# A decoder layer on one core: linear attention's steps in another order, output weights centred on GpSimd, the first middle norm computed in pairs 0 and 4 of the last batch

## The chip, the cores and the metric

The kernel runs as one launch on 1 core of one Trainium2 chip. The metric is the device time of that core in microseconds (us), the median of three runs. Engines are named as in the profile: PE is TensorE's matmul side and PEld its weight load, DVE is VectorE, ACT is ScalarE, POOL is GpSimd, SP is SyncE, which here issues most DMAs (its DMA queue stands as SPq in the rows).

## The reference, cut to what matters

One decoder layer with three blocks, each followed by a layer norm without gain or bias; x is 8 batches of 512 tokens with 256 features, float32.

```python
def linear_attention(x):                 # chunks of C = 32 tokens
    Q, K, V = x @ W_q.T, x @ W_k.T, x @ W_v.T
    S = einsum('bncd,bnkd->bnck', Qc, Kc) * mask      # decay ** (i - j) for i >= j
    O = einsum('bnck,bnkd->bncd', S, Vc).reshape(B, T, D)
    return sigmoid(x @ W_g.T) * O @ W_o.T + x

def cross_attention(x, ctx):             # 16 heads of 64
    qw, kw, vw = x @ Wq + bq, ctx @ Wk + bk, ctx @ Wv + bv
    a = softmax(where(key_mask, qw @ kw.T / sqrt(64), -inf))
    return (a @ vw) @ Wo + bo

def bitlinear(x, w):                     # ternary weights
    scale = clip(mean(abs(w), axis=1, keepdims=True), 1e-05)
    return x @ (clip(round(w / scale), -1, 1) * scale).T

def ffn(x):                              # hidden 1024, low rank 16
    h = bitlinear(x, w_fc) + gate * (x @ v.T @ fast_b.T @ u.T)
    return bitlinear(relu(h) ** 2, w_proj)

x = layernorm(x + linear_attention(x))
x = layernorm(x + cross_attention(x, ctx))
x = layernorm(x + ffn(x))
```

## The kernel before

Features stand on the 128 partitions (two tiles of 128, `DK` = 2) and the 512 tokens of a batch on the free axis, so most tiles are 128x512 or 128x1024. Products of float32 quality are made of three products of rounded parts (`_hi`, `_lo`: a CAST gives the high part, a subtraction the low one). PSUM is used as eight banks of 128x512, `ps[:, 0]` to `ps[:, 7]`. Every engine runs its own hand-written program, in the order in which its calls stand in the code; semaphores with counts are the only link between them. Nothing is scheduled by a planner.

The program has three stages.

**Linear attention**, to about 170 us. Query and key weights are folded into one matrix M, so that scores are x M x. PE runs `step(b)` once a batch: gates of b (`gates`), query side (`queries`), output projection of b - 1 (`outputs`), `scores`, `values`, the mean of b - 1 (`mean`: a product with a matrix of 1/256), `attend` (chunk products into the banks QO), and the variance of b - 1 (`variance`). In `step` of DVE stand: `finish_y` (y = 2x + attention, two operations by feature tile, and their sum `tile_sum`), `mask_scores`, `subtract_mean`, `sum_squares`, `split_x` (x of b + 1 into x_hi, x_lo), `gated` (gate times attention, then split), `root` and `scale_x1` (the norm of b - 1). ACT has `front(b)` (sigmoid of the gates, then the copies `qm` of the query side), `square`, `values` (the copies `v_tok` out of PSUM, in two halves) and `deviation` (logarithm, exponential, square: the estimate of the root). The sigmoid stands in another table of ACT than those three, so each step has two table loads. SP loads x of batch b once y of b - 2 has freed its buffer, and stores x1 of earlier batches. POOL splits the weights of the next stage and makes the effective feed-forward weight in two halves (L399 to L403).

Into these steps the weights of the feed-forward are mixed: `scales` needs the sums of absolute weights (`psc`, `scale`) and the products of `scale_means` (L748 to L758 on PE), `low_rank`, `compare_in` and `compare_out` follow in single steps. `psc` is the reduction of the output weight, 128x256<-128x2048 (its row names the shared buffer `wfc`). PE waits for a small copy of DVE for `low_rank` (`f_mid`) ahead of step 1.

**Cross attention**, about 170 to 1125 us: 8 batches of 8 pairs of heads (`PAIRS` = 8, `HALF` = 4), some 12 us a pair. In pair g PE makes `key_scores` of g in four tiles of 128 keys, the maxima's scores of g + 1 (`max_scores`), `weighted_values`, `sums` of g - 1, and keys and queries two pairs ahead. ACT makes the exponentials, the copies `pvc` and the high parts, DVE the maxima (`nmx`), reciprocals and low parts, POOL the sums over the key tiles (`acc`, `acc_hi`, `acc_lo`). `project` multiplies four pairs with the output weight; it stands in pair 4 for pairs 0 to 3 and in pair 0 of the next batch for pairs 4 to 7, and DVE's `projected_out` adds the residual. The output weight `wo` is centred once, at the start of the stage: a reduction to `wo_sum` and one subtraction, both on DVE (L1242 to L1245), and split by POOL in pairs 1 and 4 of the first batch (`split_output_weight`). `first_maxima` are the maxima of the very first pair.

**Feed-forward**, about 1125 to 1316 us. `class` members with a 2 in the name make the middle norm: `norm2_square`, `sum_squares2`, `var2_first` (the variance product of batch 0, in bank 2), `norm2_root`, `root2`, `scale2`, `split2_hi` and `split2_lo` (its output cx_hi, cx_lo). For batch 0 these stand in the last batch of cross attention: square and sum in pair 2, the rest in pair 6. `weights_hi` and `weights_lo` split the feed-forward weight, `ternary` (POOL, L184) casts the ternary output weight. `rs` at L225 is the first operation of `root2`, and PE waits for it ahead of `key_scores(g, p, 1)` of the last pair, since it frees bank 2. The rest of cross attention (`last_sums`, `last_reciprocal`, `last_attended_hi`, `last_attended_lo`, `last_project`, `last_projected`) stands between the hidden tiles of feed-forward batch 0. Each batch has eight hidden tiles on four banks (`hidden`), and then `project` over them.

The only thing that sets this order is the code of the steps. `attend` waits for both value copies (`v_out`), which ACT makes behind `square(b - 1)`; the sigmoid of b waits for `gate_used`, which DVE's gate product (L576) signals.

## Time and profile before

| | |
|---|---|
| median of 3 runs | 1316.46 us (1314.57 to 1319.1) |
| the profiled execution | 1318.03 us, its span 1315.9 us, mean granted clock 0.986 |
| PE busy | 1272.9 us, 6836 instructions |
| DVE busy | 923.5 us |
| ACT busy | 794.7 us |
| POOL busy | 775.7 us |
| HBM | 32 GB/s over the span |

The span is what the profiler sees from the first to the last instruction; the execution's own time is 2.1 us longer.  [...]

### The profile page before, as it was taken

Reading aid. Unit: us, or ns where it says so; the run is one execution under the profiler, and the core shown is the slowest. Engines: PE = TensorE matmul, PEld = TensorE weight load, DVE = VectorE, ACT = ScalarE, POOL = GpSimd, SP = SyncE. Lnnn points to the kernel's source line nnn. Section 1 sums busy time; section 2 is a strip of 40 time slices with the busy share of each in tenths; the row PEclk is TensorE's granted clock in tenths of the full one; section 3 lists DMA queues with packets and bytes.
Section 4 is the critical chain, followed back from the end, with each engine's and each line's share of the span. In section 5 each row is a group of like instructions: output and inputs, shape, how many; then the busy total and the mean of one; then the engine's idle time right before and its main releaser. Section 6 shows DMA issues by size and latency. Waiting matters only on the chain.

```text
span 1315.9 us, 21104 instructions
## 1 busy us (share of the span) xinstructions
PE 1272.9 (97%) x6836; PEld 850.6 (65%) x6836; DVE 923.5 (70%) x1809; ACT 794.7 (60%) x1063; POOL 775.7 (59%) x449
## 2 busy tenths in 40 slices
PE   6999999999999999999999999999999998899997
PEld 5767765657566656665666666657566655577775
DVE  6678876684766677576757656684775677678887
ACT  2354445574656566565657565575666666679885
POOL 3504218995877687677958767794876787300000
PEclk9999998999999999999999999999999999899998
DMA  6311211100100110011011001100200110010101
GB/s 214 113 35 62 82 47 20 19 2 17 42 11 1 32 34 0 16 32 18 0 28 37 2 0 48 18 0 16 48 2 0 33 33 2 20 61 33 64 17 48
DMA packets 99392, 43.08 MB, mean 33 GB/s; under 512 B 77169, under 2 KB 82049, under 8 KB 99345
## 3 DMA queue, kind: packets, MB, share of 16 engines
q1 hardware_dynamic: 98528, 39.33, 12.1%
q0 software_dynamic: 816, 3.15, 0.7%
q8 instruction: 27, 0.44, 0.1%
q14 instruction: 21, 0.16, 0.0%
HBM read 29.59 MB, written 12.58 MB: 32 GB/s over the span
## 4 chain that ended last, share of the span: by engine, by line
PE 89%; POOL 3%; DVE 3%; ACT 2%; issue 1%; SPq 1%; DMA 1%; POOLq 0%; ACTq 0%; DVEq 0%
PE ps L1310 16%; PE ps L1285 14%; PE ps L48 11%; PE ps L50 10%; PE ps L49 10%; PE ps L1301 4%; PE ps L1289 4%; PE ps L1343 2%; PE ps L1344 2%; PE ps L1342 2%; PE ps L1319 2%; PE ps L1732 2%; PE ps L1733 2%; POOL acc L931 2%; PE ps L716 1%
## 5 line engine op out<-in xcount | busy, mean ns | idle before, releaser
L1139 DVE CUSTOM_DVE_ANT_0 junk<-ps,mask 128x512 bf16<-128x512 f32 x504 | 314.9, 686 | 89.3 <-PE ps L1301 88.0
L1005 ACT ACTIVATE prob<-ps,mcol 128x1024 f32<-128x1024 f32 x256 | 282.0, 1116 | 140.1 <-PE ps L1289 135.2
L931 POOL TENSOR_TENSOR acc<-acc,prob 128x1024 f32<-128x1024 f32 x128 | 307.0, 2399 | 11.6 <-ACT prob L1005 0.3
L928 POOL TENSOR_TENSOR acc<-prob 128x1024 f32<-128x1024 f32 x64 | 155.3, 2426 | 220.8 <-ACT prob L1005 219.5
L1310 PE MATMUL ps<-prob,v_b 128*64 128x512 f32 x1024 | 246.2, 602 | 0.0
L945 POOL TENSOR_TENSOR acc_lo<-acc,acc_hi 128x1024 f16<-128x1024 f32 x64 | 138.7, 2168 | 5.1
L1310 PEld LDWEIGHTS ps<-prob,v_b 128*64 128x64 f32 x1024 | 68.1, 137 | 108.8 <-issue 75.9
L1285 PE MATMUL ps<-q_hi,k_hi 64*128 64x512 f32 x512 | 115.1, 445 | 4.2 <-DVE rs L225 4.0
L1301 PE MATMUL ps<-k_hi,q_hi 64*128 64x512 f32 x504 | 101.0, 396 | 3.8 <-DVE nmx L1139 3.8
L1285 PE MATMUL ps<-q_hi,k_lo 64*128 64x512 f32 x512 | 102.3, 395 | 0.0
L1285 PE MATMUL ps<-q_lo,k_hi 64*128 64x512 f32 x512 | 102.1, 394 | 0.0
L1289 PE MATMUL ps<-shift,ones_r 64*128 64x512 f32 x512 | 102.0, 394 | 0.1
L1150 DVE TENSOR_TENSOR ps<-ps,recip 128x512 f32<-128x512 f32 x64 | 44.6, 697 | 67.6 <-ACT recip L1020 67.6
L1012 ACT ACTIVATE pvc<-ps 128x512 f32<-128x512 f32 x64 | 38.3, 599 | 81.2 <-PE ps L1310 81.1
L1285 PEld LDWEIGHTS ps<-q_hi,k_hi 64*128 64x128 f32 x512 | 48.4, 185 | 55.4 <-issue 27.0
L1163 DVE SCALAR_TENSOR_TENSOR att_lo<-ps,bv,att_hi 128x512 fp32r<-128x512 f32 x64 | 48.0, 751 | 48.7 <-ACT att_hi L1028 48.7
L1173 DVE SCALAR_TENSOR_TENSOR q_lo<-ps,bq,q_hi 128x512 fp32r<-128x512 f32 x64 | 48.0, 751 | 30.3 <-ACT q_hi L1036 29.6
L1042 ACT ACTIVATE v_b<-ps 128x512 f32<-128x512 f32 x64 | 38.3, 598 | 50.0 <-PE ps L50 50.0
L1036 ACT ACTIVATE q_hi<-ps,bq 128x512 fp32r<-128x512 f32 x64 | 44.1, 688 | 37.5 <-PE ps L50 37.4
L941 POOL CAST acc_hi<-acc 128x1008 f16<-128x1008 f32 x64 | 65.4, 1022 | 0.0
L1028 ACT ACTIVATE att_hi<-ps,bv 128x512 fp32r<-128x512 f32 x64 | 44.1, 689 | 33.3 <-DVE ps L1158 33.3
L1301 PEld LDWEIGHTS ps<-k_hi,q_hi 64*128 64x128 f32 x504 | 47.8, 185 | 19.0 <-DVE nmx L1139 4.9
(230 smaller groups left out, 2881.9 us busy)
## 6 DMA issues: line engine op xcount, KB each, us to landing
shift<-nmx SPq DMA_DIRECT2D x512, 0.5 KB, 2.0
x_in<-in_xT SPq DMA_DIRECT2D x8, 512.0 KB, 3.7
x_scratch<-x_a SPq DMA_DIRECT2D x8, 512.0 KB, 2.8
raw<-in_cT SPq DMA_DIRECT2D x8, 512.0 KB, 3.7
raw<-x_scratch SPq DMA_DIRECT2D x8, 512.0 KB, 3.9
y<-x_scratch SPq DMA_DIRECT2D x8, 512.0 KB, 3.7
y_scratch<-y SPq DMA_DIRECT2D x8, 512.0 KB, 2.8
y_c<-y_scratch SPq DMA_DIRECT2D x8, 512.0 KB, 3.8
```

What stands on the lines that cost most here:

```text
L48: pe.matmul(out, lh, rh, start=(i == 0), stop=False)
L49: pe.matmul(out, lh, rl, start=False, stop=False)
L50: mm = pe.matmul(out, ll, rh, start=False, stop=(i == n - 1))
L928: pool.tensor_tensor(total, prob[:, 0], prob[:, 1], ALU.add).then_inc(acc_out, 1)
L931: pool.tensor_tensor(total, total, prob[:, kt], ALU.add).then_inc(acc_out, 1)
L945: pool.tensor_tensor(acc_lo[:], acc[:], acc_hi[:], ALU.subtract).then_inc(sum_lo_out, 1)
L1005: act.activation(prob[:, i].rearrange("p h t -> p (h t)"), SCORE[i % 2].rearrange("p h t -> p (h t)"), ACT.Exp, scale=SCALE, bias=mcol[:, ...
L1139: dve.tensor_tensor_reduce(junk[:, t % 2, h], SMAX[t % 2][:, h], mask[:], -1.0, -LOWEST, ALU.add, ALU.min, nmx[:, p % 2, t, h:h + 1]).then ...
L1285: pe.matmul(banks[:, h], l[OWN[h], par, cols], r[OWN[h], par], start=(n == 0), stop=False)
L1289: mm = pe.matmul(banks[:, h], ones_r[OWN[h], :], shift[OWN[h], par], start=False, stop=True)
L1301: mm = pe.matmul(SMAX[t % 2][:, h], q_hi[OWN[h], par, toks], k_hi[OWN[h], par], start=True, stop=True)
L1310: mm = pe.matmul(PV[OWN[h], :], v[:, kt, cols], prob[:, kt, h, :], start=(kt == 0), stop=(kt == NT - 1))
```

## The change

No product is added or removed. What moves:

- **Linear attention, PE.** The first gates are made in three parts as x_hi, then x_lo are there (`first_gates`). `variance(b - 2)` stands behind the gates of step b; `scale_means` goes from behind step 1 into step 2, between gates and queries. Values come in two halves, (0, 1) and (2, 3), and `attend` takes the first half of its tiles when the first half of the value copies is there. The wait for `f_mid` goes from ahead of step 1 to ahead of its `mean`.
- **Linear attention, ACT.** `front` keeps the sigmoid alone, followed at once by the load of the other table; then `deviation(b - 2)`, the query copies, the values, and last the square.
- **Linear attention, DVE.** `root(b - 2)` opens the step, `scale_x1(b - 2)` and `split_x(b + 1)` come behind `mask_scores`, ahead of `subtract_mean`. The reduction `psc` (`sum_out_weights`) goes from ahead of step 1 into step 1, behind `gated(1)`. Stores of x1 come one batch later.
- **First pair.** The reduction `wo_sum` and the new `wo_mean` go between the second and the third `first_maxima`; the subtraction is made by POOL in two halves (`centre_output_weight`), and the first half of the weight is split ahead of batch 0.
- **Last batch.** `weights_hi`, `weights_lo`, `norm2_square` and `sum_squares2` of feed-forward batch 0 go to pair 0, `var2_first`, `norm2_root`, `root2`, `scale2` and `split2_hi` to pair 4, `split2_lo` to the last pair. The variance uses bank 3; its buffers are separate tiles (`first_sq`, `first_sum`, `first_rs`), and PE waits for `rs2_out` in pair 5. `ternary` goes from pair 6 to the last pair.
- **Feed-forward batch 0.** `last_sums` stands behind hidden tile 4, `last_project` behind the first four tiles of the first projection; `last_project` uses banks 3 and 6.

```diff
-        self.STAT2_FIRST, self.STAT2, self.STAT3 = ps[:, 2, :], ps[:, 0, :], ps[:, 5, :]
+        self.STAT2_FIRST, self.STAT2, self.STAT3 = ps[:, 3, :], ps[:, 0, :], ps[:, 5, :]
...
                 act.wait_ge(gate_used, b)
             act.activation(gate[:], G, ACT.Sigmoid).then_inc(g_out, 1)
+            if not (isinstance(b, int) and b < 2):
+                act.preload_act_table_set("natural_log_exp_and_others")
...
-            if not (isinstance(b, int) and b == 0):
-                act.preload_act_table_set("natural_log_exp_and_others")
...
-        values(0)
+        front(1)
+        query_copies(1)
         act.wait_ge(f_sum, 1)
         act.activation(wabs[:].rearrange("p k (j n) -> p (k j) n", n=D), wpr[:], ACT.Abs).then_inc(f_abs, 1)
-        front(1)
+        values(1)
         square(0)
-        values(1)
-        deviation(0)
         with act.Fori(2, B - 1, 2) as i:
...
                 front(b)
+                deviation(b - 2)
+                query_copies(b)
+                values(b)
                 square(b - 1)
-                values(b)
-                deviation(b - 1)
...
+        la.deviation_late = lambda: deviation(B - 2)
...
         def step(b, par, last):
+            if b > 1:
+                root(b - 2)
             finish_y(b - 1, 1 - par)
             mask_scores(b)
+            if b > 1:
+                scale_x1(b - 2)
+            if not last:
+                split_x(b + 1, 1 - par)
             subtract_mean(b - 1)
             sum_squares(b - 1)
-            if not last:
-                split_x(b + 1, 1 - par)
             gated(b)
             if b == 1:
+                sum_out_weights()
                 scales()
             if b in (2, 3):
                 low_rank(b - 2)
-            if not last:
-                root(b - 1)
-                scale_x1(b - 1)
             if b in (3, 4):
                 compare_in(b - 3)
             if b in (5, 6):
...
+        split_x(1, 1)
         mask_scores(0)
-        split_x(1, 1)
-
+        gated(0)
         dve.wait_ge(f_abs, 1)
         dve.tensor_tensor(scale[:], wabs[:, 0], wabs[:, 1], ALU.add).then_inc(f_sum, 1)
-        gated(0)
         dve.wait_ge(f_mid_ps, 1)
         dve.tensor_copy(mid[:], ST[0:RANK, 0:D]).then_inc(f_mid, 1)
-        dve.wait_ge(f_abs, 2)
-        dve.tensor_reduce(psc[:], wabs[:].rearrange("p k (j n) -> p n (k j)", n=D), AX.X, ALU.add).then_inc(f_sum, 1)
...
-                for t in range(NT):
-                    mm = pe.matmul(QO[:, m, t * P:(t + 1) * P], v[:, t, m * P:(m + 1) * P], s[:, t],
-                                   start=True, stop=True)
+            for n in range(2):
+                pe.wait_ge(v_out, 2 * b + n + 1)
+                for m in range(DK):
+                    for t in (2 * n, 2 * n + 1):
+                        mm = pe.matmul(QO[:, m, t * P:(t + 1) * P], v[:, t, m * P:(m + 1) * P], s[:, t],
+                                       start=True, stop=True)
                 mm.then_inc(o_ps, 1)
...
+        def first_gates():
+            for l, r, ready in ((w_hi, x_hi, 1), (w_lo, x_hi, 1), (w_hi, x_lo, 2)):
+                pe.wait_ge(x_split, ready)
+                for m in range(DK):
+                    for k in range(DK):
+                        mm = pe.matmul(G[:, m], l["WgT"][:, k, m * P:(m + 1) * P], r[:, 0, k],
+                                       start=(l is w_hi and r is x_hi and k == 0), stop=(r is x_lo and k == DK - 1))
+            mm.then_inc(g_ps, 1)
...
+        first_gates()
...
+        pe.wait_ge(w_in, 32)
+        values(0, 0, (0, 1))
         scores(0, 0)
-        pe.wait_ge(w_in, 32)
-        values(0, 0, range(NT))
+        values(0, 0, (2, 3))
...
+            if b > 1:
+                variance(b - 2)
+            if b == 2:
+                scale_means()
             queries(b, par)
             if b == 2:
...
@@ -735,11 +770,15 @@
                 pe.wait_ge(f_low, b - 2)
             outputs(b - 1)
             scores(b, par)
-            values(b, par, (0,))
+            values(b, par, (0, 1))
+            if b == B - 1:
+                values(b, par, (2, 3))
+            if b == 1:
+                pe.wait_ge(f_mid, 1)
             mean(b - 1)
...
-            variance(b - 1)
 
...
-        pe.wait_ge(f_mid, 1)
         for b in range(1, B):
             step(b, b % 2)
-            if b == 1:
-                scale_means()
...
+        def centre_output_weight(half):
+            rows = slice(half * HALF, half * HALF + HALF)
+            means = wo_mean[:, rows].rearrange("p (k o) -> p k o", o=1).to_broadcast([P, HALF, D])
+            pool.wait_ge(wo_summed, 2)
+            pool.tensor_tensor(wo[:, rows], wo[:, rows], means, ALU.subtract).then_inc(wo_centred, 1)
+
...
-                if first and p in (1, HALF):
-                    split_output_weight(p // HALF)
+                if first and p == HALF:
+                    split_output_weight(1)
...
-                if last and p == PAIRS - 2:
+                if last and p == PAIRS - 1:
...
+        centre_output_weight(0)
+        pool.wait_ge(la.y_out, 2 * B)
+        split_output_weight(0)
+        centre_output_weight(1)
...
-                    f.norm2_square(act, 0, 0)
-                if last and p == PAIRS - 2:
-                    f.weights_hi(act)
...
-                if last and p == PAIRS - 2:
-                    f.norm2_root(act, 0, True)
...
+                if last and p == 0:
+                    f.weights_hi(act)
+                    f.norm2_square(act, 0, 0)
+                if last and p == HALF:
+                    f.norm2_root(act, 0, True)
...
+        la.deviation_late()
...
-                    f.weights_lo(dve, 0)
+                if last and p == PAIRS - 1:
+                    f.split2_lo(dve, 0, 0)
...
+                if last and p == 0:
+                    f.weights_lo(dve, 0)
+                    f.weights_lo(dve, 1)
+                    f.sum_squares2(dve, 0, True)
                 if p == 0 and not first:
...
+                    projected_out(b - 1, 1)
+                if last and p == HALF:
+                    f.root2(dve, 0)
+                    projected_out(b, 0, (0,))
+                    f.scale2(dve, 0, 0)
+                    projected_out(b, 0, (1,))
+                    f.split2_hi(dve, 0, 0)
+                elif p == HALF:
...
+        first_maxima(1)
+        dve.tensor_reduce(wo_sum[:], wo[:], AX.X, ALU.add).then_inc(wo_summed, 1)
+        dve.wait_ge(wo_summed, 1)
+        dve.tensor_scalar(wo_mean[:], wo_sum[:], 1.0 / D, None, ALU.mult).then_inc(wo_summed, 1)
+        first_maxima(2)
+        first_maxima(3)
         la.root(B - 1)
         la.scale_x1(B - 1)
-        dve.tensor_reduce(wo_sum[:], wo[:], AX.X, ALU.add).then_inc(wo_centred, 1)
-        dve.wait_ge(wo_centred, 1)
-        dve.scalar_tensor_tensor(out=wo[:], in0=wo_sum[:].rearrange("p (k o) -> p k o", o=1).to_broadcast([P, PAIRS, D]),
-                                 scalar=-1.0 / D, in1=wo[:], op0=ALU.mult, op1=ALU.add).then_inc(wo_centred, 1)
...
-                if last and p == PAIRS - 1:
+                if last and p == HALF + 1:
                     pe.wait_ge(f.rs2_out, 1)
...
-                if last and p == PAIRS - 2:
-                    f.var2_first(pe)
...
+                if last and p == HALF:
+                    f.var2_first(pe)
...
+            for i in (2, 3, 4):
+                hidden(b, i, first)
+            if first:
+                ca.last_reciprocal_estimate()
+            hidden(b, 5, first)
             if first:
                 ca.last_attended_hi()
-            for i in (3, 4, 5):
...
-            if first:
-                ca.last_reciprocal()
...
             hidden_lo(b, 2)
-            if first:
-                ca.last_attended_lo()
...
+            if first:
+                ca.last_reciprocal()
             hidden_lo(b, 5)
             if first:
-                ca.last_projected()
+                ca.last_attended_lo()
...
+                if first:
+                    ca.last_projected(0)
                 f.scale2(dve, b + 1, 1 - par)
             hidden_lo(b, 6)
+            if first:
+                ca.last_projected(1)
...
-            if first:
-                ca.last_sums()
-            for i in (1, 2, 3):
+            for i in (0, 1, 2, 3):
...
             if first:
+                ca.last_sums()
...
-            if first:
-                ca.last_project()
...
             if first:
-                pe.wait_ge(ca.o_out, 2 * DK * B)
...
+                for m in range(DK):
+                    project(b, m, range(0, 4))
+                pe.wait_ge(f.relu_out, 6)
+                ca.last_project()
+                for m in range(DK):
+                    project(b, m, range(4, 6))
...
+            if first:
+                pe.wait_ge(ca.o_out, 2 * DK * B)
```

Three places, by the order of the instructions on an engine. First DVE, one step of linear attention (b = 3): `x_hi`, `x_lo` are the split of x, `dev_a` the mean subtraction, `tile_sum_a<-sq_a` the sum of squares, `sq_a<-ps,gate` the gate product, `rs_a` the root. Before:

```order
L523 SCALAR_TENSOR_TENSOR y_a<-x_in,ps 128x512 x2
L528 TENSOR_TENSOR tile_sum_a<-y_a 128x512
L547 TENSOR_TENSOR s_masked<-ps,dmask 128x512
L541 TENSOR_TENSOR dev_a<-y_a,ps 128x1024
L533 TENSOR_TENSOR tile_sum_a<-sq_a 128x512
L481 CAST x_hi<-x_in 128x1024
L483 TENSOR_TENSOR x_lo<-x_in,x_hi 128x1024
L576 TENSOR_TENSOR sq_a<-ps,gate 128x1024
L578 CAST og_hi<-sq_a 128x1024
L580 TENSOR_TENSOR og_lo<-sq_a,og_hi 128x1024
```

With the change, from the root of the batch before the last:

```order
L571 SCALAR_TENSOR_TENSOR rs_a<-ps,eps,inv_a 128x512
L574 SCALAR_TENSOR_TENSOR rs_a<-rs_a,est_a 128x512
L539 SCALAR_TENSOR_TENSOR y_a<-x_in,ps 128x512 x2
L544 TENSOR_TENSOR tile_sum_a<-y_a 128x512
L563 TENSOR_TENSOR s_masked<-ps,dmask 128x512
L581 SCALAR_TENSOR_TENSOR x_a<-dev_a,rs_a 128x1024
L497 CAST x_hi<-x_in 128x1024
L499 TENSOR_TENSOR x_lo<-x_in,x_hi 128x1024
L557 TENSOR_TENSOR dev_a<-y_a,ps 128x1024
L549 TENSOR_TENSOR tile_sum_a<-sq_a 128x512
L592 TENSOR_TENSOR sq_a<-ps,gate 128x1024
L594 CAST og_hi<-sq_a 128x1024
```

The split of x stands ahead of the mean subtraction instead of behind the sum of squares, and the root ahead of y instead of behind the gate product.

Second POOL, at the start of cross attention; `bx` is the split input, `acc` the sum over key tiles of the first pair. Before:

```order
L985 CAST bx_hi<-raw 128x1024
L949 TENSOR_TENSOR bx_lo<-raw,bx_hi 128x1024
L988 MEMSET shift 128x1024
L928 TENSOR_TENSOR acc<-prob 128x1024
L931 TENSOR_TENSOR acc<-acc,prob 128x1024 x2
```

With the change:

```order
L1031 CAST bx_hi<-raw 128x1024
L989 TENSOR_TENSOR bx_lo<-raw,bx_hi 128x1024
L1034 MEMSET shift 128x1024
L999 TENSOR_TENSOR wo<-wo,wo_mean 128x1024
L1004 CAST wo_hi<-wo 128x1024
L1006 TENSOR_TENSOR wo_lo<-wo,wo_hi 128x1024
L999 TENSOR_TENSOR wo<-wo,wo_mean 128x1024
L968 TENSOR_TENSOR acc<-prob 128x1024
```

Four operations on the output weight stand ahead of the first sum.

Third DVE in the last batch of cross attention: `x`, `x_even` is the output of the middle norm, `cx_hi`, `cx_lo` its split. Before, from the low weights in pair 6 on, into its norm:

```order
L1150 TENSOR_TENSOR ps<-ps,recip 128x512
L1152 SCALAR_TENSOR_TENSOR ps<-ps,recip 128x512
L1158 SCALAR_TENSOR_TENSOR ps<-pvc,ps 128x512
L1163 SCALAR_TENSOR_TENSOR att_lo<-ps,bv,att_hi 128x512
L180 TENSOR_TENSOR wfc_lo<-wfc,wfc_hi 128x1024
L225 SCALAR_TENSOR_TENSOR rs<-ps,eps,inv 128x512
L228 SCALAR_TENSOR_TENSOR rs<-rs,est 128x512
L238 SCALAR_TENSOR_TENSOR x<-y_c,rs 128x1024
L245 CAST cx_hi<-x 128x1024
L249 TENSOR_TENSOR cx_lo<-x,cx_hi 128x1024
```

With the change, in pair 4:

```order
L1218 SCALAR_TENSOR_TENSOR k_lo<-ps,bk,k_hi 128x512
L1223 SCALAR_TENSOR_TENSOR q_lo<-ps,bq,q_hi 128x512
L240 SCALAR_TENSOR_TENSOR first_rs<-ps,eps,first_sq 128x512
L243 SCALAR_TENSOR_TENSOR first_rs<-first_rs,first_sq 128x512
L1234 SCALAR_TENSOR_TENSOR y<-ps,bo_centred,y 128x512
L253 SCALAR_TENSOR_TENSOR x_even<-y_even,first_rs 128x1024
L1234 SCALAR_TENSOR_TENSOR y<-ps,bo_centred,y 128x512
L260 CAST cx_hi_even<-x_even 128x1024
```

The norm lies between the two additions of the projection's result; nothing of it but the last subtraction (`split2_lo`) is left for the last pair.

## Rows read from the trace of the kernel before

**Rows 1.** Page, part 1: busy us, share of the span, instructions.

```profile
PE 1272.9 (97%) x6836; PEld 850.6 (65%) x6836; DVE 923.5 (70%) x1809; ACT 794.7 (60%) x1063; POOL 775.7 (59%) x449
```

**Rows 2.** Waits of PE, whole span: waiting, awaited: total us, times, longest.

```profile
PE ps L716 <- ACT v_tok L437: 7.1, 8, 1.0
...
PE ps L1285 <- DVE rs L225: 4.0, 1, 4.0
PE ps L1301 <- DVE nmx L1139: 3.8, 2, 2.9
PE ps L48 <- issue: 3.5, 1, 3.5
...
PE ps L1319 <- DVE att_lo L1163: 1.9, 1, 1.9
PE ps L1319 <- POOL acc_lo L945: 1.7, 1, 1.7
...
PE ps L48 <- DVE cx_lo L249: 1.4, 1, 1.4
```

**Rows 3.** Windows after waits: length, busy of PE, PEld, DVE, ACT, POOL, PEclk, DMA.

```profile
198.00:206.00 8.00, 7.07 (x24) 3.07 (x26) 4.63 (x16) 1.11 (x1) 7.50 (x5) 0.57 0.13 10
1115.00:1121.00 6.00, 5.90 (x28) 4.36 (x30) 5.93 (x3) 3.02 (x4) 6.00 (x3) 0.59 0.01 3
1131.00:1138.00 7.00, 6.59 (x18) 4.94 (x19) 3.78 (x6) 4.77 (x8) 0.35 (x1) 0.57 0.00 0
```

**Rows 4.** Timeline, start of linear attention: start us, duration us, instruction.

```profile
30.22 3.83 DVE L640 TENSOR_REDUCE psc<-wfc 128x256 f32<-128x2048 f32 x1
...
50.15 1.88 PE L753 MATMUL ps<-scale,mean_w 128*128 128x512 f32 x4
```

**Rows 5.** Timeline of SP: issues of x for batches 3, 6 and 7.

```profile
62.00 0.39 SPq L360 DMA_DIRECT2D x_in<-in_xT  x1
...
121.78 0.38 SPq L360 DMA_DIRECT2D x_in<-in_xT  x1
...
139.85 0.38 SPq L360 DMA_DIRECT2D x_in<-in_xT  x1
```

**Rows 6.** Tile x_in, all its loads.

```profile
DMA to landing us min/median/max: 3.3/3.7/8.3
```

**Rows 7.** Timeline of DVE, inside one step of linear attention.

```profile
128.09 0.68 DVE L481 CAST x_hi<-x_in 128x1024 fp32r<-128x1024 f32 x1
128.81 1.23 DVE L483 TENSOR_TENSOR x_lo<-x_in,x_hi 128x1024 fp32r<-128x1024 f32 x1
129.95 1.22 DVE L576 TENSOR_TENSOR sq_a<-ps,gate 128x1024 f32<-128x1024 f32 x1
...
133.85 0.69 DVE L558 SCALAR_TENSOR_TENSOR rs_a<-rs_a,est_a 128x512 f32<-128x512 f32 x1
```

**Rows 8.** Timeline of ACT, the same step.

```profile
125.69 1.06 ACT L432 ACTIVATE sq_a<-dev_a 128x1024 f32<-128x1024 f32 x1 [6.88 <-DVE dev_a L541]
...
131.51 0.63 ACT L448 ACTIVATE est_a<-inv_a 128x512 f32<-128x512 f32 x1
...
132.82 1.28 ACT L421 ACT_TABLE_LOAD   x1
```

**Rows 9.** Timeline near 102 us: DVE beside POOL's weight step.

```profile
102.20 2.35 POOL L401 TENSOR_TENSOR wfc_raw<-wfc_raw,scale 128x1024 f32<-128x1024 f32 x1
102.26 2.83 DVE L528 TENSOR_TENSOR tile_sum_a<-y_a 128x512 f32<-128x512 f32 x1
```

**Rows 10.** Timeline of DVE, the first pair's maxima and the reduction.

```profile
187.15 0.69 DVE L1145 CUSTOM_DVE_ANT_0 junk<-ps,mask 128x512 bf16<-128x512 f32 x1 [2.54 <-PE ps L1295]
...
193.05 2.28 DVE L1242 TENSOR_REDUCE wo_sum<-wo 128x8 f32<-128x2048 f32 x1
```

**Rows 11.** Timeline, last batch: ACT in pair 0, POOL in pair 6.

```profile
1035.01 4.68 ACT L1005 ACTIVATE prob<-ps,mcol 128x1024 f32<-128x1024 f32 x4 [5.88 <-PE ps L1289]
...
1116.13 2.35 POOL L184 CAST tern_r<-tern 128x2048 fp32r<-128x2048 bf16 x1
```

171 lines of the change are left out of this document (87 added, 84 removed).

## The prediction

> **What bounds the kernel now.** I read the page first: TensorE (PE) is busy for 97% of the span [rows 1], so only its idle time and its slow time can be won. Second, the waits of PE [rows 2]: 7.1 us in eight waits of 0.9 us for the value copies of linear attention, 3.5 us once at the start ("issue": PE stood at the semaphore f_mid), 2.9 of the 3.8 us for `nmx` at the first pair, 0.9 of them in pair 3 of the last batch, 4.0 us for `rs` in the last pair, and 1.4, 1.9 and 1.7 us at the start of the feed-forward stage. Between the first pair and the last batch PE never waits, and that code is unchanged. [...] Busy time times (1 - clock) is what each costs: 7.07 x 0.43 = 3.0 us after the first-pair wait, 5.90 x 0.41 = 2.4 after the wait for `rs`, 6.59 x 0.43 = 2.8 after the feed-forward waits. Waits of 0.9 us leave the clock alone.
>
> The change has three parts that can be summed apart.
>
> **Linear attention, start.** The first gates begin on x_hi alone, copies come before the weight means, and PE no longer stands at f_mid: by the measured durations PE gets to its second attend some 7 us sooner. But the reduction of the output weights moves from before step 1 to behind `gated(1)`, and `scale_means` needs it. It takes 3.83 us [rows 4]. It now starts after y of batch 0 (by the same durations at about 33 us), the load of x for batch 2 (3.8 us with its issue, [rows 5, 6], more if it shares the DMA engines with the 1 MB weight load that GpSimd starts at that time), its split (2.0), mean subtraction, square and sum (3.1), `gated` (3.3): about 46 us, and ends at about 50. Before, `scale_means` began at 50.15 [rows 4]. So PE arrives early and waits some 6 us there, then runs slowly for a while (2 us, like those of [rows 3]). What it has then already done (2.75 us of gates) pays for that: outputs(1) ends some 0.5 us sooner than before. I take -0.5, range -2.5 to +1.
>
> **Linear attention, the loop.** The 0.9 us wait goes: values are copied before the square, and attend takes them in halves. PE alone would then need 18.07 - 0.9 = 17.2 us a step, 18.07 being the distance of two x loads [rows 5]. But the new order closes a ring through four engines, which I sum from y(b-1) to y(b). The x load, 3.8 us from its release to its landing ([rows 6] has 3.7 over all loads, from the issue); split of x, now ahead of the mean subtraction, 0.68 + 1.23; subtraction 1.22 like the op of its size; square 1.06 on ScalarE; sum 0.69; gate product 1.22 [rows 7, 8]: with hand-overs 10.0 us. The sigmoid table load carries the wait for `gate_used` in the new order as in the old, and stood clear of it before. Now it comes right at it: table 1.28, sigmoid 1.05 like the square of its size, the second table 1.28, then deviation(b-1), three functions of 0.63 [rows 8], 5.6 us. Then root's two and the two y operations, 0.69 each, 2.8 us [rows 7]. The ring is 18.4 us, longer than PE's 17.2, and longer than the 18.07 of before. PE's wait moves from attend to scores (query copies stand behind the deviation).
> Two rounds hold a low-rank product on PE (1.8 us, like the mean products of [rows 4]). The first is PE's: 19.0. In the next three GpSimd's weight steps get into the ring. [rows 9] shows the price: a 0.69 us sum lasted 2.83 us, until GpSimd's 2.35 us operation beside it had ended. Two-input SBUF operations of the ring (root's second, tile_sum, scale_x1) now meet such operations, 1.3 to 1.6 us a round: 19.7, 20.0, 20.0. The last is 18.5. The same four rounds took 139.85 - 62.00 = 77.9 us before [rows 5]; now 78.7; with the fifth +1.3 us. In the last step there is no x load and the ring is open: its value-copy wait of 0.9 us goes [rows 2], and GpSimd's splits of the next stage's inputs, which held its gate split, are over sooner, worth 0.9 more (half of one hold as in [rows 9]): -1.8. Linear attention together: -0.5 + 1.3 - 1.8 = **-1.0**, range -9 (ring never binds: five rounds at PE's pace) to +4 (twice the holds).
>
> **First pair.** Reduction (2.28 us) and means go into VectorE's idle 2.54 us before the third maximum [rows 10], and the 2.3 us subtraction to GpSimd. The maxima are due 4.6 us earlier, which would remove 2.9 us of wait and the 3.0 us of clock. But GpSimd now runs about 8 us of subtraction and splitting just while VectorE does root's second operation and scale_x1. By [rows 9] each can be held for one GpSimd operation: up to 3 us, so the maxima start 1.1 instead of 4.6 us earlier and 1.9 us of wait stay. [...] I take the middle of 0 and 1.9: 1.0 us of wait and half of the clock loss. **-5.9 + 2.5 = -3.4**, range -5.9 to -1.
>
> **Last batch and feed-forward.** Weights, square and sum go to pair 0. There ScalarE is idle for 5.88 us while PE projects [rows 11]; they need 3.1. VectorE gets 3.2 us more before the y additions; the first ends about when PE asks for its bank: 0 to 0.3 us. In pair 4 the variance product costs PE 0.9 us (half of the two-product row in [rows 4]), the same that it saves in pair 6; root and scale hide behind the 24 products of the projection. Gone: 0.9 + 4.0 + 1.4 + 1.9 + 1.7 = 9.9 us of waits, 5.2 us of clock. What is late next: with no product ahead of it the last pair waits 0.8 us for the `pvc` copy, and its second score tile 0.8 us for att_lo of the pair before, both formerly hidden; exponentials pace the short pair (0.5). GpSimd ends its sums about 6.6 us after PE has begun the hidden tiles; the ternary copy, 2.35 us [rows 11], comes right behind. VectorE's hidden_lo and sum_squares2 have only SBUF inputs and alternate with them, so PE stands at var2(1): 0.5 us if nothing is held, 3.1 if twice. I take 2.4. The last projection then starts with its inputs ready, and batch 1 follows without a wait. **-15.1 + 4.5 = -10.6**, range -13.5 to -6.5 (the clock falls once more).
>
> **Sum.** -1.0 - 3.4 - 10.6 = -15.0. The profiled execution took 1318.03 us (span 1315.9), 1.6 above the median; it would be 1303.0, and against the median 1316.46 - 15.0 = **1301.4 us**.
>
> **Rivals.**
> (A) The ring doesn't bind, because loads land in 3.3 us and sigmoid's table is loaded while waiting: linear attention gives -8 instead of -1: 1294. For it: 18.4 against 17.2 is only 1.2 us, half of it hand-overs. Against: each piece is a measured row.
> (B) Holds and clock cost more: a fresh slow stretch in the last pair or at var2 (2.4 to 2.8 us), the first pair keeps its wait, linear attention loses 3: 1309.
> (C) Both ends go ideally and (A) holds: 1288.
> (D) Slower: the x load is now inside the ring at its start. Where it takes 8.3 us, the longest of [rows 6], every one of five rounds is 4.6 us longer, +23: 1325. It turns into a loss above 3.7 + 15/5 = 6.7 us a load. Against it: the loads inside the loop stand near the median, and the store of x1 is released behind the load, by scale_x1.
> (E) The change doesn't do what it says: the last pair still waits for `rs`, since VectorE's root in pair 4 stands ahead of the y addition and is late: gain 9 us instead of 15, 1308.
>
> **How the numbers follow.** Chances: forecast 0.45 (own range 1297 to 1306), A 0.20, B 0.18, C 0.05, D 0.05, E 0.07. The range 1291 to 1311 leaves out C, D and the tail of B. About 0.3% (4 us) is what a measurement can tell from no change: faster than 1312.5 are the forecast, A, C, E and most of B, 0.90; the same 0.05 (B's tail); slower 0.05 (D).
>
> **What would show it.** In the changed profile: x loads in steps 4 to 6 spaced 18.4 us or more (right) or 17.2 (A); PE idle before the score products of linear attention and none before attend; one wait of 5 to 7 us at `scale_means`; sigmoid's table load right at the end of the gate product. At the first pair a wait for `nmx` under 2 us. No wait for `first_rs`; in the last pair two waits of 0.8 us; a wait of up to 3 us at var2 and none for `acc_lo`. Wrong would be: a new wait in pairs 0 or 4 of the last batch, or x loads above 5 us.

## The result and the profile after

The changed kernel took 1303.66 us (median of 4 runs, 1303.37 to 1304.39), beside 1317.78 us of the kernel before in the same comparison (4 runs, 1314.57 to 1320.26). The ratio is 0.9895, with a 95% interval of 0.9876 to 0.9914: 1.1% faster. Forecast were 1301.4 us in a range of 1291 to 1311. The profiled execution of the changed kernel took 1303.37 us and has a span of 1301.3 us, 14.6 less than before.

The first part of its page answers to [rows 1]:

```profile
PE 1266.9 (97%) x6836; PEld 846.6 (65%) x6836; DVE 922.9 (71%) x1809; ACT 793.6 (61%) x1061; POOL 779.5 (60%) x451
```

The same products keep PE busy for 6.0 us less, since fewer of them run at the low clock (mean granted clock 0.993 instead of 0.986). Low is 0.50 here: from 198.5 to 204.5 us every window of 1 us of the kernel before has a granted clock of 0.50, and every one of the changed kernel has 1.00. The waits of PE in the changed kernel (waiting, awaited: total us, times, longest us) answer to [rows 2]:

```profile
PE ps L792 <- DVE psc L651: 6.1, 1, 6.1
...
PE ps L1765 <- issue: 3.1, 1, 3.1
PE ps L57 <- ACT qm L441: 2.8, 3, 1.0
...
PE ps L48 <- DVE og_lo L596: 2.0, 1, 2.0
...
PE ps L1356 <- DVE nmx L1189: 1.3, 1, 1.3
...
PE ps L1340 <- issue: 0.7, 1, 0.7
...
PE ps L1340 <- DVE att_lo L1213: 0.5, 1, 0.5
PE ps L1340 <- ACT prob L1055: 0.3, 1, 0.3
```

Gone are the value copies, `f_mid`, `rs`, `cx_lo`, the `att_lo` and `acc_lo` of the last sums. New are 6.1 us for the reduction `psc`, three waits for the query copies `qm` where there was one, 3.1 us at the variance of feed-forward batch 1 (L1765), and 1.6 us in the last pair. The wait for `og_lo`, at the end of linear attention, has grown from 1.1 to 2.0 us. The clock behind the waits, in windows of the changed kernel (stretch, length, busy PE, PEld, DVE, ACT, POOL, granted clock, DMA share, GB/s), answers to [rows 3]:

```profile
48.00:56.00 8.00, 7.42 (x25) 5.00 (x26) 3.63 (x6) 0.88 (x2) 3.10 (x4) 0.77 0.38 133
...
197.00:204.00 7.00, 7.00 (x34) 3.67 (x34) 2.66 (x9) 2.58 (x4) 6.70 (x5) 1.00 0.33 77
...
1123.00:1131.00 8.00, 7.54 (x24) 5.53 (x25) 5.79 (x9) 7.24 (x13) 0.00 (x0) 0.79 0.00 0
```

Behind the 1.3 us wait at the first pair the clock is whole (1.00). Behind the waits of 6.1 and 3.1 us it falls once more, for 7.42 x 0.23 = 1.7 us and 7.54 x 0.21 = 1.6 us.

I divided the two spans at four products that both kernels have: the first key score of cross attention, the same product of the second pair, the first of the last batch, and the end.

| stretch | before | after | difference | forecast |
|---|---|---|---|---|
| linear attention, to the first key score | 192.05 | 190.04 | -2.0 | -1.0 |
| the first pair | 17.92 | 13.44 | -4.5 | -3.4 |
| pairs between, unchanged code | 806.46 | 806.83 | +0.4 | 0 |
| last batch and feed-forward | 299.5 | 291.0 | -8.5 | -10.6 |
| span | 1315.9 | 1301.3 | -14.6 | -15.0 |

The times of the products come from the timeline of PE; the last batch begins at 1016.43 and at 1010.31 us.

The first line of the table has a scatter as large as itself. Six traces (this one and five of the experiments below) have the changed kernel's linear attention: the first key score stands between 190.0 and 192.4 us in them, 191.0 in the mean. Two have the old one, at 192.05 and 194.25. There are two sources. One is the start: the first product of `outputs(1)` comes at 55.5 to 58.4 us in the six. The other is the clock. Behind the 2.0 us wait for `og_lo` it stays whole in this trace and in one other; in the remaining four it falls (0.79 from 167 to 175 us in each), the changed kernel run again among them. The window from 167 to 175 us, in this trace and in that of the second run:

```profile
167.00:175.00 8.00, 6.27 (x30) 5.21 (x30) 6.76 (x10) 2.90 (x5) 0.00 (x0) 1.00 0.00 0
```

```profile
167.00:175.00 8.00, 6.25 (x20) 5.01 (x21) 5.24 (x8) 1.99 (x4) 0.00 (x0) 0.79 0.00 0
```

From the scores of step 7 to the first key score it is 35.0 us in the two traces with the whole clock and 36.6 to 36.7 in the four others.

### The profile page after: what moved, and what is told of

Same layout as the page of the kernel before. It is cut to its first block, busy times and chain, and to the rows that moved or that the text cites. A ratio compares the mean times of both kernels' runs of the same rounds, so it can differ in the third digit from the quotient of the medians.

```text
span 1301.3 us, 21071 instructions
## 1 busy us (share of the span) xinstructions
PE 1266.9 (97%) x6836; PEld 846.6 (65%) x6836; DVE 922.9 (71%) x1809; ACT 793.6 (61%) x1061; POOL 779.5 (60%) x451
## 4 chain that ended last, share of the span: by engine, by line
PE 87%; DVE 5%; ACT 3%; issue 2%; POOL 2%; DMA 1%; SPq 0%; DVEq 0%; ACTq 0%; POOLq 0%
PE ps L1365 17%; PE ps L1340 15%; PE ps L48 10%; PE ps L50 9%; PE ps L49 9%; PE ps L1356 4%; PE ps L1344 4%; PE ps L1397 2%; PE ps L1398 2%; PE ps L1399 2%; PE ps L1374 2%; PE ps L1790 2%; PE ps L1791 2%; PE ps L57 1%; DMA x_in<-in_xT 1%
## 5 line engine op out<-in xcount | busy, mean ns | idle before, releaser
L1068 ACT ACTIVATE recip<-ps 128x512 f32<-128x512 f32 x64 | 38.1, 596 | 34.5 <-PE ps L1374 34.5
```

## Experiments

What I held: linear attention's step is a ring through four engines, VectorE operations with two SBUF inputs are held by GpSimd operations beside them, and the long waits also cost clock. The rivals were that PE's own products pace the step, and that the long VectorE operations had other reasons. All edits below are to the changed kernel.

**The changed kernel again**, for the level.

> The changed kernel once more, unaltered, as the level for the runs beside it. Expected 1303.7 us again (its four runs lay between 1303.4 and 1304.4). The stage times read from its first trace should come again: x loads 19.2 to 19.6 us apart in steps 4 to 7, 6.1 us of wait at the weight means, 1.3 us for nmx at the first pair, 3.1 us at the variance of feed-forward batch 1.

It took 1304.29 us (1303.57 to 1306.18; ratio to the kernel before 0.9885, 0.9869 to 0.9902); the waits in its trace are those expected. Its first key score stands at 191.62 us, 1.6 later than in the first trace.

**The sigmoid's table ahead of its waits.**

```diff
         def front(b):
 
+            if not (isinstance(b, int) and b < 2):
+                act.preload_act_table_set("sigmoid_and_others")
             act.wait_ge(g_ps, b + 1)
```

> One edit to the changed kernel: ScalarE loads the sigmoid's table at the end of the step before, ahead of the waits for the gates and for the gate product, so that the load (1.28 us) lies in its idle 2.2 us. Ring theory (linear attention's step is a ring y, load and split of x, mean subtraction, square, sum, gate product, table, sigmoid, table, estimate of the root, root, y): the table leaves the ring, each of the steps 3 to 7 is 1.2 us shorter, x loads 18.2 us apart, the waits for the query copies (0.9 us each) go, total 5 to 6 us less, about 1298. Rival (TensorE's own products pace the step, the ring only touches it): loads stay 19.5 us apart and the total stays at 1303.7. Second rival (holds by GpSimd pace the step): the gain is made in steps without GpSimd work only, 2 us.

It took 1305.18 us (1303.12 to 1307.05; ratio 0.9892, 0.9874 to 0.9911): no gain. The expected 5 to 6 us are refuted, and the number is that of the first rival, by which TensorE's own products pace the step; the next two runs decide on it. The x loads of SP (start us, us) still stand 19.5 us apart:

```profile
97.95 0.37 SPq L369 DMA_DIRECT2D x_in<-in_xT  x1
...
117.42 0.37 SPq L369 DMA_DIRECT2D x_in<-in_xT  x1
...
136.87 0.37 SPq L369 DMA_DIRECT2D x_in<-in_xT  x1
```

The table did leave the ring: its load stands behind the square, at 126.36 us, and the root starts right behind the two compares and the estimate. First the DVE, then the POOL rows of that trace:

```profile
131.58 1.23 DVE L626 SCALAR_TENSOR_TENSOR wpr_raw<-psc,wpr_raw 128x1024 f32<-128x1024 f32 x1
132.91 0.75 DVE L573 SCALAR_TENSOR_TENSOR rs_a<-ps,eps,inv_a 128x512 f32<-128x512 f32 x1
133.70 1.95 DVE L576 SCALAR_TENSOR_TENSOR rs_a<-rs_a,est_a 128x512 f32<-128x512 f32 x1
...
132.95 2.15 POOL L419 TENSOR_TENSOR tern<-tern,wpr_raw 128x1024 bf16<-128x1024 bf16 x1 [11.78 <-DVE wpr_raw L626]
```

The compare at 131.58 releases GpSimd's operation at 132.95, and VectorE's next operation with two SBUF inputs, the root's second, lasts 1.95 instead of 0.69 us, until GpSimd's has ended. These 1.26 us are what the table had cost (1.28). In the changed kernel the table load kept the root away from that operation: the root's second starts at 134.96 us, with GpSimd's operation at 132.94 to 135.09, and lasts 0.69.

**GpSimd's weight steps cut to 8 columns.** The effective feed-forward weight is left out but for 8 columns of each half, so this time is that of a kernel with 15 us less work on GpSimd (six operations of 2.15 to 2.70 us).

```diff
-            pool.tensor_tensor(wfc[:, k], above[:, k], wfc[:, k], ALU.subtract).then_inc(f_step, 1)
+            pool.tensor_tensor(wfc[:, k, 0:8], above[:, k, 0:8], wfc[:, k, 0:8], ALU.subtract).then_inc(f_step, 1)
...
-            pool.tensor_tensor(wfc[:, k], wfc[:, k], scale[:], ALU.mult).then_inc(f_step, 1)
+            pool.tensor_tensor(wfc[:, k, 0:8], wfc[:, k, 0:8], scale[:, 0:8], ALU.mult).then_inc(f_step, 1)
...
-            pool.tensor_tensor(c["wfc"][:, k], c["wfc"][:, k], wfc[:, k], ALU.add).then_inc(f_step, 1)
+            pool.tensor_tensor(c["wfc"][:, k, 0:8], c["wfc"][:, k, 0:8], wfc[:, k, 0:8], ALU.add).then_inc(f_step, 1)
```

> The changed kernel with GpSimd's six steps of the effective feed-forward weight (three operations of 128x1024 in each of two halves, in steps 4 to 6 of linear attention) cut to 8 columns each: the feed-forward weight is then wrong in the other columns, the output too. Hold theory: the operations of VectorE that lasted 1.5 and 2.8 us beside them (sum of y, x1) take 0.7 and 1.2 us again, the split of x then waits for its load instead, and the loads of steps 5 and 6 stand 18.4 us apart instead of 19.5 (the ring of the forecast without holds). Rival (VectorE's own work or TensorE paces the step, the holds lie in slack): 19.5 stays, within 0.3.

One run, 1301.33 us. The loads of SP in this kernel are 18.39 and 18.40 us apart, the ring of the forecast to a hundredth or two:

```profile
99.57 0.37 SPq L369 DMA_DIRECT2D x_in<-in_xT  x1
...
117.96 0.37 SPq L369 DMA_DIRECT2D x_in<-in_xT  x1
...
136.36 0.37 SPq L369 DMA_DIRECT2D x_in<-in_xT  x1
```

The same operations of VectorE, first in the changed kernel, where GpSimd's weight steps run at 115.69 to 121.15 us:

```profile
117.41 1.53 DVE L544 TENSOR_TENSOR tile_sum_a<-y_a 128x512 f32<-128x512 f32 x1
118.86 0.68 DVE L563 TENSOR_TENSOR s_masked<-ps,dmask 128x512 f32<-128x512 f32 x1
119.46 2.77 DVE L581 SCALAR_TENSOR_TENSOR x_a<-dev_a,rs_a 128x1024 f32<-128x1024 f32 x1
122.16 0.68 DVE L497 CAST x_hi<-x_in 128x1024 fp32r<-128x1024 f32 x1
```

and then with the small steps:

```profile
117.97 0.69 DVE L544 TENSOR_TENSOR tile_sum_a<-y_a 128x512 f32<-128x512 f32 x1
118.58 0.68 DVE L563 TENSOR_TENSOR s_masked<-ps,dmask 128x512 f32<-128x512 f32 x1
119.18 1.21 DVE L581 SCALAR_TENSOR_TENSOR x_a<-dev_a,rs_a 128x1024 f32<-128x1024 f32 x1
121.63 0.69 DVE L497 CAST x_hi<-x_in 128x1024 fp32r<-128x1024 f32 x1 [1.24 <-DMA x_in<-in_xT]
```

The two operations with two SBUF inputs are short again, `s_masked`, which reads PSUM, never was long, and the split of x now waits 1.24 us for its load: the load is in the ring. PE does not pace these steps: it still waits 0.44 and 0.97 us in them for the query copies. That settles the holds and the ring against the rivals, by the trace of one run.

**Both edits together.**

> The same cut of GpSimd's weight steps together with the early load of the sigmoid's table. Moving the table alone left the loads 19.5 us apart: the root's second operation then took 1.95 us instead of 0.69, beside GpSimd's first weight step, which VectorE's compare had just released. If that hold is what took the table's 1.28 us, both edits together give 17.2 to 17.5 us a step in steps 5 and 6 (18.4 less the table, or TensorE's own pace of 17.2). Rival (a ring through something else, as the compare operations on VectorE, which my sum left out: 2.45 us): 18.0 us or more.

One run, 1301.76 us. The step between the loads at 100.12 and 117.25 us took 17.13 us, and PE is busy for all of them: its own pace. The next, up to 135.26, took 18.01: beside GpSimd's ternary step, which was not cut, the root's second operation lasted 1.80 us instead of 0.69:

```profile
132.25 1.80 DVE L576 SCALAR_TENSOR_TENSOR rs_a<-rs_a,est_a 128x512 f32<-128x512 f32 x1
```

So the table does leave the ring where no operation of GpSimd stands ready to take its place. The total doesn't show it: from the load at 99.57 us to the first key score the kernel with the small steps alone takes 88.51 us, and this one, from its load at 100.12, takes 88.47. The 1.6 us won are still there when the output products of the last batch start (65.51 us behind the load, against 67.15). Then the clock takes them: behind a wait of 2.02 us for `og_lo` it falls in this trace (0.72 from 165 to 171 us, 5.37 x 0.28 = 1.5 us), where in the other it stays whole (1.00) behind a wait of 1.97 us.

**The reduction of the output weights earlier.**

```diff
             mask_scores(b)
+            if b == 1:
+                sum_out_weights()
             if b > 1:
                 scale_x1(b - 2)
...
             if b == 1:
-                sum_out_weights()
                 scales()
```

> One edit to the changed kernel: the reduction of the output weights (3.8 us on VectorE) stands behind mask_scores(1), ahead of the split of x for batch 2, instead of behind gated(1). VectorE has 1.9 us of idle time there (it waits for the x load). If the 6.1 us wait at the weight means is only the reduction's place, it goes, about 0.6 us appear at the gates of batch 2, and with it goes the low clock behind it (1.8 us by the window behind the wait); the second product of the output projection starts up to 5 us sooner: total 5 to 7 us less, 1297 to 1299. Rival: TensorE is early there anyway and the next late thing (og_lo of batch 1, then VectorE's scales ahead of the next y) takes the place: 1 to 2 us gained, 1302.

It took 1298.56 us (1296.80 to 1301.76; ratio 0.9849, 0.9830 to 0.9867), 5.7 less than the changed kernel beside it. PE has no wait at the weight means any more, and its clock is whole there (window of this kernel):

```profile
38.00:60.00 22.00, 21.86 (x107) 17.17 (x106) 18.50 (x20) 8.91 (x12) 13.70 (x11) 1.00 0.35 132
```

The reduction starts at 36.42 us and lasts 3.74; 1.9 us of that lie in time in which VectorE had stood waiting for the x load. The 6.1 us wait came from its place in the queue.

**The variance product behind hidden tile 6.**

```diff
-            if not last:
+            if not (first or last):
                 var2(b + 1)
             hidden(b, par, 5, first)
             hidden(b, par, 6, first)
+            if first:
+                var2(b + 1)
```

> One edit to the changed kernel: in feed-forward batch 0 the variance product of batch 1 stands behind hidden tile 6 instead of behind tile 4. Hold theory (VectorE's two low parts take 4.4 us since GpSimd's last sum and the ternary cast run beside them; the sum of squares is ready at 1123.4 us of the trace): TensorE has two tiles more to do (2.9 us), the 3.1 us wait shrinks to under 0.5 us, and the low clock behind it (2 us) goes too: 1303.7 - 5 = 1299. Rival (the hidden tiles themselves wait for the relu copies, which start late as ScalarE waits for the sums): the wait only moves into the tiles, gain under 1 us.

It took 1299.83 us (1299.57 to 1300.26; ratio 0.9851, 0.9835 to 0.9867), 4.5 less. The 3.1 us wait is gone, one of 0.4 us for the last `h_lo` came, and the window from 1120 to 1132 us has the whole clock (1.00) where the changed kernel has 0.86.

**The ternary cast behind the sum.**

```diff
                     pool.wait_ge(q_ps, PAIRS * B)
+                    pool.wait_ge(f.sq2_sum_out, 2)
                     f.ternary(pool)
```

> The changed kernel with one more wait on GpSimd: the cast of the ternary weight starts only when the sum of squares of batch 1 is done. It releases the ternary weight later, at about 1124 of the trace; TensorE needs it at 1127 or later. Hold theory: VectorE's two low parts are then held by the last acc_lo operation alone (until 1119.9), the sum comes at about 1121.9 instead of 1123.4, and TensorE's wait at the variance is 1.6 us instead of 3.1; with so short a wait the clock may hold. Rival (the low parts are slow for another reason, as their inputs): the wait stays at 3.1.

One run, 1301.42 us, and a wait of 1.4 us instead of 3.1. VectorE's two low parts in the changed kernel, and below them the two operations of GpSimd:

```profile
1118.34 4.42 DVE L1641 TENSOR_TENSOR h_lo<-relu,h_hi 128x512 fp32r<-128x512 f32 x2 [3.30 <-ACT relu L1568]
1122.68 0.68 DVE L229 TENSOR_TENSOR sq_sum<-sq 128x512 f32<-128x512 f32 x1
...
1117.77 2.15 POOL L985 TENSOR_TENSOR acc_lo<-acc,acc_hi 128x1024 f16<-128x1024 f32 x1
1119.86 2.35 POOL L198 CAST tern_r<-tern 128x2048 fp32r<-128x2048 bf16 x1
```

and with the cast behind the sum:

```profile
1119.20 2.73 DVE L1642 TENSOR_TENSOR h_lo<-relu,h_hi 128x512 fp32r<-128x512 f32 x2 [3.32 <-ACT relu L1569]
1121.85 0.68 DVE L229 TENSOR_TENSOR sq_sum<-sq 128x512 f32<-128x512 f32 x1
```

I read the 4.42 us as two holds, one for each operation of GpSimd; with the cast moved one is left. Behind a wait of 1.4 us the clock stays whole (1.00 from 1120 to 1132 us).

**The first centring and split in pairs 1 and 2.**

```diff
-        centre_output_weight(0)
-        pool.wait_ge(la.y_out, 2 * B)
-        split_output_weight(0)
-        centre_output_weight(1)
...
+                if first and p == 1:
+                    centre_output_weight(0)
+                    split_output_weight(0)
+                if first and p == 2:
+                    centre_output_weight(1)
```

> The changed kernel with GpSimd's subtraction of the weight means and the first split moved out of the first pair's start: subtraction of the first half and its split in pair 1 of the first batch, second subtraction in pair 2. Hold theory: the root's second operation (2.02 us) and x1 (2.80 us) take 0.69 and 1.22 us, the maxima start 2.9 us earlier, and the 1.3 us wait for nmx goes. The second pair starts 1.3 us earlier. GpSimd's sums of pairs 1 and 2 come up to 6 us later; if TensorE then waits for acc_lo, up to 2 us are given back there. Rival (VectorE is late for another reason): the wait stays at 1.3.

One run, 1304.56 us: no gain. In the changed kernel root and x1 of the last batch last 2.02 and 2.80 us beside GpSimd's weight:

```profile
188.39 0.75 DVE L571 SCALAR_TENSOR_TENSOR rs_a<-ps,eps,inv_a 128x512 f32<-128x512 f32 x1
189.17 2.02 DVE L574 SCALAR_TENSOR_TENSOR rs_a<-rs_a,est_a 128x512 f32<-128x512 f32 x1
191.22 2.80 DVE L581 SCALAR_TENSOR_TENSOR x_a<-dev_a,rs_a 128x1024 f32<-128x1024 f32 x1
```

With the work moved they last 0.69 and 1.23 us and the wait for `nmx` is gone. But two waits for GpSimd's sums of pairs 2 and 3 come, at 233.41 and 246.20 us (waits of PE in this kernel):

```profile
PE ps L1375 <- POOL acc_lo L985: 1.6, 2, 0.9
```

1.3 us of wait won, 1.6 given back: these 8 us of GpSimd find no free place in pairs 1 and 2.

**Linear attention as before, all else as changed.** The whole function of the first stage is that of the kernel before.

> The changed kernel with the linear attention of the kernel before (start, loop and order of the steps), all else as changed. If the parts add, the two traces say what linear attention is worth: the first score product of cross attention stood at 192.1 us before and at 190.0 after, so 2.0 us are lost: 1306.3 us beside 1304.3 of the changed kernel. The maxima's wait at the first pair should be as in the changed kernel, 1.3 us. Rival (the new order of linear attention is what lets the first pair's start come early, since the last step's sums and splits lie otherwise): the wait for nmx is 2 us or more, and 3 us or more are lost.

It took 1307.18 us (1305.36 to 1309.53; ratio 0.9924, 0.9905 to 0.9943), 2.9 above the 1304.29 of the changed kernel, where 2.0 were expected and 3 or more were the rival's. The two were not in the same comparison: the kernel before took 1317.17 us in the one and 1319.66 in the other, so that against it the two differ by 5.4 us, and the range of either is 3 to 4 us. By the totals, linear attention is worth 3 to 5 us, give or take 2. In the trace the first key score stands at 194.25 us, where the six traces of the new order have 190.0 to 192.4. The trace decides on the rival: the wait for `nmx` is 1.3 us, as in the changed kernel. So the first pair's gain does not hang on the new order of linear attention.

**The centring as before.** Reduction and subtraction on VectorE behind x1, splits in pairs 1 and 4.

```diff
         first_maxima(1)
-        dve.tensor_reduce(wo_sum[:], wo[:], AX.X, ALU.add).then_inc(wo_summed, 1)
-        dve.wait_ge(wo_summed, 1)
-        dve.tensor_scalar(wo_mean[:], wo_sum[:], 1.0 / D, None, ALU.mult).then_inc(wo_summed, 1)
         first_maxima(2)
         first_maxima(3)
         la.root(B - 1)
         la.scale_x1(B - 1)
+        dve.tensor_reduce(wo_sum[:], wo[:], AX.X, ALU.add).then_inc(wo_summed, 1)
+        dve.wait_ge(wo_summed, 1)
+        dve.scalar_tensor_tensor(out=wo[:], in0=wo_sum[:].rearrange("p (k o) -> p k o", o=1).to_broadcast([P, PAIRS, D]),
+                                 scalar=-1.0 / D, in1=wo[:], op0=ALU.mult, op1=ALU.add).then_inc(wo_centred, 1)
```

> The changed kernel with the centring of the output weight as before: reduction and subtraction on VectorE behind x1, splits in pairs 1 and 4. By the traces the first pair gained 4.5 us (wait for nmx 2.94 to 1.31, low clock behind it gone): 1304.3 + 4.5 = 1308.8, a wait of 2.9 to 3.0 us for nmx, and the low clock behind it. Rival (the clock stays high whatever the wait): 1306 us.

It took 1308.22 us (1307.15 to 1309.56; ratio 0.9927, 0.9912 to 0.9943), 3.9 above the changed kernel; 1308.8 were expected. From the first key score to that of the second pair it takes 17.8 us, the changed kernel 13.4 and the kernel before 17.9. Its waits and its window:

```profile
PE ps L1347 <- DVE nmx L1179: 2.9, 1, 2.9
```

```profile
198.00:206.00 8.00, 6.76 (x24) 3.12 (x26) 4.94 (x16) 1.11 (x1) 7.50 (x5) 0.57 0.09 5
```

Behind the wait of 2.9 us the low clock is back (0.57, 6.76 x 0.43 = 2.9 us); behind the 1.3 us of the changed kernel it was 1.00 in the same window.

**Three edits together**: the early table, the early reduction, the late variance product.

> The changed kernel with three edits together: the sigmoid's table loaded early, the reduction of the output weights ahead of the split of x for batch 2, the variance product of feed-forward batch 1 behind hidden tile 6. Alone the second gave 5.7 us and the third 4.5 us, the first nothing. They lie at different places, so they should add: 1304.3 - 5.7 - 4.5 = 1294 us, 2.0% less than the kernel before. Rival: the granted clock, held high by the shorter waits, comes down elsewhere: 1297 or more.

It took 1294.67 us (5 runs, 1292.51 to 1295.04; ratio 0.9828, 0.9815 to 0.9842), 1.7% below the kernel before; 1294 were expected. That is 9 to 10 us below the changed kernel by the medians, but 7 to 8 when each is set against the kernel before in its own comparison. The mean granted clock of its trace is 0.998, beside 0.993 of the changed kernel. The largest waits of PE in it, behind that for the first load:

```profile
PE ps L57 <- DVE y_a L541: 2.7, 3, 0.9
PE ps L1868 <- DVE y_sum L1729: 2.0, 1, 2.0
PE ps L48 <- DVE og_lo L598: 2.0, 1, 2.0
```

## Why the prediction was right, and where not

The sum was right: 14.6 us by the spans, 14.1 by the medians, 15.0 forecast. That it is so close is luck. The start, the first rounds of the loop and the first pair gave some 4.2 us more than forecast; the fifth round, the end of linear attention, the pairs between and the last batch gave some 4.7 us less. Most of the mechanisms stood as they were told; that of the end of linear attention did not. The numbers below are those of the two profiled executions.

- **The ring.** Forecast were 18.4 us for a step without holds; with GpSimd's small steps it is 18.39 and 18.40. With holds, rounds of 19.0, 19.7, 20.0 and 20.0 us were forecast, and from load to load the changed kernel took 19.2, 19.55, 19.48 and 19.48 (59.16 to 136.88 us, 77.7 instead of 78.7). The holds came to 1.1 us a round, not 1.3 to 1.6: `tile_sum` was 0.84 and x1 1.56 us longer, less the 1.24 us for which the split of x would else have waited for its load. The root's second operation, which the forecast counted among the held, lasted 0.69 us in the two rounds of 19.48. The round of 19.55 us was PE's, which is busy for all of it. Rival A (the ring doesn't bind) fell. The fifth round took 1.0 us more than before, not 0.5; its load of x came 5.1 us after its issue.
- **What the ring's sum left out.** After the gate product VectorE has 2.45 us of compares in steps 3 to 6 ahead of the root. They run beside ScalarE's tables and so cost nothing in the changed kernel (they end at 132.79 us, and the root waits 1.39 us for ScalarE's estimate, until 134.18), but the second of them releases the GpSimd operation that then holds the root, and so the early table brought nothing. Taking a link out of this ring did not shorten it by the length of that link.
- **The start** gave 2.7 us (outputs(1) starts at 55.52 instead of 58.22), not 0.5. The mechanism was right: a wait of 6.1 us for the reduction, "some 6" forecast, then 1.7 us of clock. But the reduction ended at 48.5 instead of 50 us: the steps ahead of it took 1.2 us less than summed, and it lasted 3.76 us. The means of the six new and two old traces (56.5 and 59.2 us) give 2.7 us too.
- **The end of linear attention** gave 0.1 us, not 1.8; in the four traces in which the clock falls behind the wait for `og_lo`, it loses 1.5. This was the wrong step. From the scores of step 7 to the first key score it is 35.04 us, before 35.13. The value-copy wait went, but PE waits 1.96 instead of 1.07 us for `og_lo`. By the trace the gate product starts 1.5 us after `attend` has ended (163.15 to 164.64 us), where it started at once before (166.08 and 166.11). The sum of squares and the gate product, with the change and before:

```profile
163.81 0.69 DVE L549 TENSOR_TENSOR tile_sum_a<-sq_a 128x512 f32<-128x512 f32 x1 [1.13 <-ACT sq_a L447]
164.64 1.22 DVE L592 TENSOR_TENSOR sq_a<-ps,gate 128x1024 f32<-128x1024 f32 x1
```

```profile
162.97 1.69 DVE L533 TENSOR_TENSOR tile_sum_a<-sq_a 128x512 f32<-128x512 f32 x1 [1.12 <-ACT sq_a L432]
166.11 1.22 DVE L576 TENSOR_TENSOR sq_a<-ps,gate 128x1024 f32<-128x1024 f32 x1 [1.46 <-PE ps L716]
```

The product stands behind the sum of squares on VectorE, and that came late, because in the last step the new order puts the mean behind all four value tiles on PE (160.34 us), not between them. The forecast summed this step as an open ring and left that place out. This is read from the two traces; no run moves the mean. GpSimd's splits of the next inputs did come sooner, by 5.5 us (155.09 instead of 160.64), but their memset then held the gate's cast for 0.83 us.

- **The first pair** gave 4.5 instead of 3.4 us. The two holds are there (1.33 and 1.58 us, 2.9 together, "up to 3" forecast), the wait is 1.3 us, where the sum had taken 1.0 (the middle of 0 and 1.9), and the clock loss is gone whole (1.00 from 197 to 204 us) instead of by half. That 0 and that half were my estimates, which no run shows; what the runs show is a wait of 1.3 us and no loss behind it. The 3.0 us of clock in this sum, like the 5.2 in that of the last batch, are busy time x (1 - clock) from the windows of [rows 3], at 0.57, 0.59 and 0.57.
- **The last batch** gave 8.5 instead of 10.6 us. All five waits went, with their clock, and no wait for `first_rs` came. The last pair has waits of 0.7, 0.5 and 0.3 us (2.1 forecast, 1.6 found). At the variance PE waits 3.1 us, which is the forecast's "3.1 if twice"; I had taken 2.4. And I put no clock behind it in the sum, though a wait of 2.9 us had cost clock in [rows 3]: 1.6 us. 15.1 - 1.6 - 3.1 - 1.6 = 8.8. Two runs show how the wait at the variance arises; but no run puts the last batch's order back, so that these 8.5 us, the largest part of the gain, rest on the traces before and after alone.
- **The other rivals.** Of B the slow stretch behind the variance came, and the rest did not. C fell with A, and D and E fell: the loads of x took 3.6 us in the median, and no wait for `first_rs` came.

Which operations were held shows beside GpSimd's work on the output weight in the changed kernel: the root's second operation and x1, with two SBUF inputs, lasted 2.02 and 2.80 us, 0.69 and 1.23 with that work moved away; maxima with one SBUF input lasted 0.69 us beside GpSimd's subtraction of the weight means (at 185.14 and 185.75 us, the subtraction from 185.09 to 186.99). The two `h_lo` took 2.73 instead of 4.42 us, 1.69 less, when one of the two GpSimd operations beside them was moved away.

## What to carry to other kernels

Once waits are moved, ask what each releases: here a compare freed a GpSimd operation that held the very next VectorE operation with two SBUF inputs (1.95 instead of 0.69 us), which ate the 1.28 us won ahead of it. A long wait on PE has a second price: those of 2.9 to 6.1 us in the midst of its work were followed here by 1.3 to 3.0 us lost to the low clock, those of 1.3 and 1.4 us standing alone by none (granted clock 1.00), and so were the five of 0.9 us for the value copies from 60 to 160 us in the kernel before (1.00 over that stretch). Three waits of 1.4, 1.9 and 1.7 us within some 7 us cost 2.8. A wait of 2.0 us went either way: the same code behind it ran at 1.00 in one trace of a kernel and at 0.79 in another, some 1.5 us longer. So compare two traces of one kernel before a difference of 1.5 us is put down to an edit. A long reduction belongs where its engine already waits for a load, not behind the work that the busiest engine needs next: the one of 3.7 us gave 5.7 us when it was moved so.

## What was not expected of the hardware

Four things, with their numbers. The holds show as length of the VectorE operation, not as idle time before it: 4.42 us for two `h_lo`, whose median over the 64 of the changed kernel is 0.69, and the profile counts all of it as work of DVE (busy for 4.34 of the 4.34 us from 1118.34 to 1122.68). A cast was held too: in the changed kernel the `og_hi` of the last step, 128x1024 with one SBUF input, took 1.52 us, where the median of its eight is 0.69, beside a GpSimd memset at 165.92 to 166.87 us (the cast's own row begins at 165.89). The sigmoid's table load took 1.28 us on ScalarE in the changed kernel (128.49 to 129.77, the sigmoid at 129.79); in the kernel with the early table, where it lies in idle time (at 126.36 us), the sigmoid starts 0.09 us after the gate product has ended. And the clock behind one and the same wait of 2.0 us is not the same in every execution: whole in two of the six traces with the changed kernel's linear attention (1.00 from 167 to 175 us), low in four (0.79), 1.6 us apart.
